# Attention plus feed-forward layer on eight cores: the step between the two halves is split into a statistics pass and a transpose pass

## The reference

```python
x = x + _layernorm(_L0_attn_ref(_layernorm(x), A_l, r_l, B_l, C_l))
x = x + _layernorm(_L0_ffn_ref(_layernorm(x), gate_w, up_w, down_w, ...))

# attention, D = 256 rows of X, the rest Y; N = 2048
U = B_l @ X;  W = C_l @ X
att = relu(U.T @ W);  att[N-1, N-1] = 0
X_out = X + A_l @ (X @ att);  Y_out = Y + r_l * (Y @ att)

# feed-forward, hidden 2048, inner 5632
g = (xf @ gate_w.T) * gate_s;  u = (xf @ up_w.T) * up_s
out = ((silu(g) * u) @ down_w.T) * down_s
```

## Time and profile before

| What | us |
|---|---|
| median of 3 runs | 1420.22 (1420.18 to 1420.74) |
| profiled execution, its own time | 1418.88 |
| its span, slowest core | 1417.3 |
| spans of the eight cores | 1410.9 to 1417.3 |

### The profile page before, as it was taken

The page is one execution under the profiler, slowest core; times in us unless marked ns, Lnnn a source line. Parts: engine busy times, 40 slices in busy tenths (PEclk is TensorE's granted clock), DMA queues, the critical chain, the costliest instruction groups (busy, mean ns, idle before and its releaser), DMA issues. The chain is left out here.

```text
span 1417.3 us, 13080 instructions; the slowest of 8 cores (1410.9 to 1417.3 us)
## 1 busy us (share of the span) xinstructions
PE 1142.3 (81%) x5236; PEld 506.6 (36%) x5236; DVE 372.8 (26%) x487; ACT 239.3 (17%) x316; POOL 46.8 (3%) x68
## 2 busy tenths in 40 slices
PE   2438989931117999999999999999999999999940
PEld 0113333310113444444444444444444444444410
DVE  2066335334330102310123001220113110231285
ACT  2302333355540000000000000000000000000045
POOL 1000000000010000000000000000000000000000
PEclk9769999975558999999999999999999999999975
DMA  6860000002129943085331935137540664303048
GB/s 113 227 129 1 1 1 0 1 30 85 65 78 171 169 87 60 0 139 100 60 60 19 160 61 91 29 59 124 94 80 1 103 124 71 60 0 60 0 141 333
DMA packets 28748, 112.86 MB, mean 80 GB/s; under 512 B 2448, under 2 KB 5008, under 8 KB 24208
## 3 DMA queue, kind: packets, MB, share of 16 engines
q0 software_dynamic: 22784, 75.24, 31.4%
q1 hardware_dynamic: 4752, 33.59, 6.5%
q10 hardware_dynamic: 1152, 3.20, 0.8%
HBM read 170.48 MB, written 16.78 MB: 132 GB/s over the span
## 5 line engine op out<-in xcount | busy, mean ns | idle before, releaser
L752 PE MATMUL ps_f<-att,gw_sb 128*128 128x512 bf16 x1408 | 313.2, 381 | 14.7 <-DMA gw_sb<-gw 14.7
L804 PE MATMUL ps_f<-dwb,hdn 128*128 128x512 bf16 x1408 | 304.9, 379 | 11.7 <-DVE hdn L782 11.7
L768 PE MATMUL ps_f<-att,uw_sb 128*128 128x512 bf16 x1408 | 311.1, 379 | 0.0
L782 DVE SCALAR_TENSOR_TENSOR hdn<-ps_f,us_sb,sg 128x1024 bf16<-128x1024 f32 x44 | 56.5, 1284 | 564.9 <-PE ps_f L768 564.9
L752 PEld LDWEIGHTS ps_f<-att,gw_sb 128*128 128x128 bf16 x1408 | 138.1, 98 | 182.5 <-issue 17.7
L804 PEld LDWEIGHTS ps_f<-dwb,hdn 128*128 128x128 bf16 x1408 | 137.3, 98 | 179.2 <-issue 14.5
L768 PEld LDWEIGHTS ps_f<-att,uw_sb 128*128 128x128 bf16 x1408 | 137.8, 98 | 166.1
L778 ACT ACTIVATE sg<-ps_f,gs_sb 128x1024 bf16<-128x1024 f32 x44 | 49.1, 1115 | 831.6 <-PE ps_f L752 831.6
L425 PE MATMUL ps_t<-att,xTb 128*128 128x512 bf16 x512 | 115.9, 384 | 35.7 <-DMA xTb<-xT 35.7
L817 DVE TENSOR_TENSOR acc<-acc,ps_f 128x2048 f32<-128x2048 f32 x40 | 91.5, 2287 | 172.1 <-PE ps_f L804 172.1
L644 PE MATMUL ps_tr<-ident_sb,xTb 128*128 128x128 bf16 x128 | 16.2, 305 | 108.8 <-ACT xTb L626 105.2
(11 more groups left out here) (104 smaller groups left out, 381.8 us busy)
## 6 DMA issues: line engine op xcount, KB each, us to landing
gw_sb<-gw POOLq DMA_DIRECT2D x22, 1024.0 KB, 8.5
uw_sb<-uw POOLq DMA_DIRECT2D x22, 1024.0 KB, 8.6
dwb<-dw POOLq DMA_DIRECT2D x11, 2048.0 KB, 28.8
xbuf<-x SPq DMA_DIRECT2D x8, 1024.0 KB, 22.4
x1sp<-xbuf SPq DMA_DIRECT2D x8, 1024.0 KB, 3.9
x1rb<-x1sp SPq DMA_DIRECT2D x8, 1024.0 KB, 16.0
y<-acc SPq DMA_DIRECT2D x8, 1024.0 KB, 6.7
xTb<-xT POOLq DMA_DIRECT2D x4, 1024.0 KB, 44.1
```

The lines of the kernel that those rows point to most:

```text
L752: e.matmul(ps_f[:, half, :], gw_sb[:, slot, ht * P:(ht + 1) * P], lnfT_v[:, ht, half * 512:(half + 1) * 512], start=(ht == 0), stop=(ht == ...
L768: e.matmul(ps_f[:, 2 + half, :], uw_sb[:, slot, ht * P:(ht + 1) * P], lnfT_v[:, ht, half * 512:(half + 1) * 512], start=(ht == 0), stop=(h ...
L782: pl.vop(lambda e, gi=gi, li=li: e.scalar_tensor_tensor(hdn[:, li, :], ps_f[:, 2:4, :], us_sb[:, gi:gi + 1], sg[:, gi % 2, :], ALU.mult, A ...
L804: e.matmul(ps_f[:, bs + hc, :], hdn[:, li, tt * P:(tt + 1) * P], dwb[:, li, hc * 512:(hc + 1) * 512], start=(li == 0), stop=(li == blk - 1)),
```

## The change

The step between the halves is taken apart.

- Part of it stays in the second block, without the quarters and without `tmpe`: for each row tile one DVE instruction over 2048 columns computes `xbuf = attn_out * rN8 + xbuf` and its row sum. The constant `ngN8` is left out there (the layernorm that follows doesn't see a constant added to a row) and is added at the end of the kernel, in the bias of the last normalization. The squares are summed as before, the stores too. The statistics `rF` and `ngF8` are made once, for all eight row tiles, after the loop.
- A new block of its own holds the rest. POOL loads the first two chunks of `gw` and `uw` at its start. ACT normalizes a row tile into one of two bf16 tiles `lnfbf`, PE transposes it in the same groups of four, and DVE alone copies all four groups out, into a tile `lnfT` of its own.
- The loads of `dsB` and `dwb` stay in the feed-forward block, which now comes after that block. The condition `blk > 2` ahead of a load holds for all rounds (the rounds have 8 or 4).
- In the fourth block `w1f` is float32 instead of bf16, and one small DVE addition is new. Tiles are placed elsewhere in SBUF and PSUM, with `gw_sb`, `uw_sb` and `lnfT` on its right side.

```diff
-    for dt in range(DT):
-        for c in range(4):
-            pl.aop(... e.activation(tmpe[:, sl, :], attn_out[:, dt, cs_], AF.Identity,
-                scale=rN8[:, dt:dt + 1], bias=ngN8[:, dt:dt + 1]), ...)
-            pl.vop(... e.scalar_tensor_tensor(
-                xbuf[:, dt, cs_], tmpe[:, sl, :], 1.0, xbuf[:, dt, cs_],
-                ALU.mult, ALU.add, accum_out=s1acc[:, dt, c:c + 1]), ...)
+    for dt in range(DT):
+        pl.vop(lambda e, dt=dt: e.scalar_tensor_tensor(
+            xbuf[:, dt, :], attn_out[:, dt, :], rN8[:, dt:dt + 1],
+            xbuf[:, dt, :], ALU.mult, ALU.add,
+            accum_out=s1acc[:, dt:dt + 1]), w=[("sAC", rn_done)])
...
-        pl.vop(lambda e, dt=dt: e.reduce_sum(t1c[:, :], s1acc[:, dt, :], ...))
...
-        pl.aop(lambda e, dt=dt: e.activation(rF[:, dt:dt + 1], lnt[:, dt:dt + 1], AF.Exp, scale=c_nh))
...
+    pl.vop(lambda e: e.tensor_scalar(muF8[:, :], s1acc[:, :], 1.0 / D, None,
+                                     ALU.mult))
+    pl.vop(lambda e: e.tensor_scalar(lnt[:, :], s2acc[:, :], 1.0 / D, None,
+                                     ALU.mult), w=[("sAC", x1sq_ac)])
...
+    pl.aop(lambda e: e.activation(lnt[:, :], lnt[:, :], AF.Ln, bias=c_eps),
+           w=[("sDV", fstat)])
+    pl.aop(lambda e: e.activation(rF[:, :], lnt[:, :], AF.Exp, scale=c_nh))
...
+    pl.new_block()
     load_chunk(0)
     load_chunk(1)
+    for dt in range(DT):
+        pl.aop(lambda e, dt=dt: e.activation(
+            lnfbf[dt % 2][:, :], xbuf[:, dt, :], AF.Identity,
+            scale=rF[:, dt:dt + 1], bias=ngF8[:, dt:dt + 1]), w=wcast)
+        for g4 in range(4):
+            for k in range(4):
+                pl.em("tensor", ... e.transpose(pb[:, k * P:(k + 1) * P],
+                                  lnfbf[dt % 2][:, nt * P:(nt + 1) * P],
+                                  ident_sb[:, :]), ...)
+            pl.vop(lambda e, dt=dt, g4=g4, pb=pb: e.tensor_copy(
+                lnfT[:, g4 * 4:g4 * 4 + 4, dt * P:(dt + 1) * P],
+                pb[:, :].rearrange("p (k c) -> p k c", c=P)), w=[("sPE", tg)])
...
+    pl.emit(nc, sems)
...
+    pl.new_block()
     pl.dma("sDS", "scalar", dsB[:, :], t_ds.ap(), w=[("sSP", SP)])
...
-    w1f = s3.enter_context(nc.sbuf_tensor("w1f", [P, DT, D], BF16))
+    w1f = s3.enter_context(nc.sbuf_tensor("w1f", [P, DT, D], F32))
...
+    pl.vop(lambda e: e.tensor_tensor(ngW8[:, :], ngW8[:, :], ngN8[:, :],
+                                     ALU.add))
```

More of the change, by code:

```diff
@@ L169, in build_nc @@
     nA2 = g_sb("nA2", [P, DT])
+    muW8 = g_sb("muW8", [P, DT])
+    rW8 = g_sb("rW8", [P, DT])
+    ngW8 = g_sb("ngW8", [P, DT])
     cst = g_sb("cst", [P, 2])
@@ L187, in build_nc @@
         nc.sbuf_tensor("amixb", [P, JT, R], BF16, side="right"))
+    sT = ExitStack()
+    attn_out = sT.enter_context(nc.sbuf_tensor("attn_out", [P, DT, D], BF16))
     s0 = ExitStack()
@@ L532, in build_nc @@
         epilogue(1)
[L534 to L540, removed]
     pl.vop(lambda e: e.reduce_sum(muN8[:, :], nacc[:, :, :],
@@ L607, in build_nc @@
[L607 to L663, removed]
@@ L667, in build_nc @@
+    fstat = pl.v("sDV")
+    pl.aop(lambda e: e.activation(lnt[:, :], lnt[:, :], AF.Ln, bias=c_eps),
+           w=[("sDV", fstat)])
+    pl.aop(lambda e: e.activation(rF[:, :], lnt[:, :], AF.Exp, scale=c_nh))
+    rf_done = pl.v("sAC")
+    pl.vop(lambda e: e.tensor_tensor(ngF8[:, :], muF8[:, :], rF[:, :],
+                                     ALU.mult), w=[("sAC", rf_done)])
+    pl.vop(lambda e: e.tensor_scalar_mul(ngF8[:, :], ngF8[:, :], -1.0))
+    ngf_done = pl.v("sDV")
     SP = pl.v("sSP")
@@ L674, in build_nc @@
     sT.close()
[L675 to L687, removed]
+    sTl = ExitStack()
+    lnfT = sTl.enter_context(nc.sbuf_tensor("lnfT", [P, HT, R], BF16,
+                                            side="right"))
+    sW2 = ExitStack()
+    gw_sb = sW2.enter_context(nc.sbuf_tensor("gw_sb", [P, 4, D], BF16,
+                                             side="right"))
+    uw_sb = sW2.enter_context(nc.sbuf_tensor("uw_sb", [P, 4, D], BF16,
+                                             side="right"))
     g_mm_done = {}
@@ L707, in load_chunk @@
         uw_ld[ci] = (usem, pl.v(usem))
+    sTx = ExitStack()
+    lnfbf = [sTx.enter_context(nc.sbuf_tensor(f"lnfbf{i}", [P, D], BF16))
+             for i in range(2)]
+    psT = ExitStack()
+    ps_tr = [psT.enter_context(nc.psum_tensor(f"ps_tr{i}", [P, 4 * P], BF16))
+             for i in range(2)]
     pl.new_block()
@@ L711, in build_nc @@
     load_chunk(1)
+    tr_done = {}
+    ev_done = {}
+    for dt in range(DT):
+        wcast = []
+        if dt >= 2:
+            wcast.append(("sPE", tr_done[dt - 2]))
+        pl.aop(lambda e, dt=dt: e.activation(
+            lnfbf[dt % 2][:, :], xbuf[:, dt, :], AF.Identity,
+            scale=rF[:, dt:dt + 1], bias=ngF8[:, dt:dt + 1]), w=wcast)
+        cast_done = pl.v("sAC")
+        for g4 in range(4):
+            pb = ps_tr[g4 % 2]
+            wt = [("sAC", cast_done), ("sXI", XI)]
+            prev = (dt, g4 - 2) if g4 >= 2 else ((dt - 1, g4 + 2)
+                                                 if dt > 0 else None)
+            if prev in ev_done:
+                wt.append(("sDV", ev_done[prev]))
+            for k in range(4):
+                nt = g4 * 4 + k
+                pl.em("tensor",
+                      lambda e, dt=dt, nt=nt, k=k, pb=pb:
+                      e.transpose(pb[:, k * P:(k + 1) * P],
+                                  lnfbf[dt % 2][:, nt * P:(nt + 1) * P],
+                                  ident_sb[:, :]),
+                      w=(wt if k == 0 else ()),
+                      inc=("sPE" if k == 3 else None))
+            tg = pl.v("sPE")
+            pl.vop(lambda e, dt=dt, g4=g4, pb=pb: e.tensor_copy(
+                lnfT[:, g4 * 4:g4 * 4 + 4, dt * P:(dt + 1) * P],
+                pb[:, :].rearrange("p (k c) -> p k c", c=P)),
+                w=[("sPE", tg)])
+            ev_done[(dt, g4)] = pl.v("sDV")
+        tr_done[dt] = pl.v("sPE")
+    pl.emit(nc, sems)
+    sTx.close()
+    sx.close()
+    psT.close()
+    s2 = ExitStack()
+    acc = s2.enter_context(nc.sbuf_tensor("acc", [P, DT, D], F32))
+    dsB = s2.enter_context(nc.sbuf_tensor("dsB", [P, D], F32))
+    s2w = ExitStack()
+    dwb = s2w.enter_context(nc.sbuf_tensor("dwb", [P, 8, D], BF16))
+    hdn = s2w.enter_context(nc.sbuf_tensor("hdn", [P, 8, R], BF16))
+    sg = s2w.enter_context(nc.sbuf_tensor("sg", [P, 2, R], BF16))
+    ps2 = ExitStack()
+    ps_f = ps2.enter_context(nc.psum_tensor("ps_f", [P, 8, MQ], F32))
+    pl.new_block()
     pl.dma("sDS", "scalar", dsB[:, :], t_ds.ap(), w=[("sSP", SP)])
@@ L727, in build_nc @@
             load_chunk(ci0)
-            load_chunk(ci0 + 1)
+            if blk > 2:
+                load_chunk(ci0 + 1)
         wdw = ([("sPE", down_mm[(bi - 1, 6)])] if bi > 0
@@ L753, in build_nc @@
                                    gw_sb[:, slot, ht * P:(ht + 1) * P],
-                                   lnfT_v[:, ht, half * 512:(half + 1) * 512],
+                                   lnfT[:, ht, half * 512:(half + 1) * 512],
                                    start=(ht == 0), stop=(ht == HT - 1)),
@@ L825, in build_nc @@
     s2w.close()
+    sW2.close()
+    sTl.close()
     s3 = ExitStack()
     x1rb = s3.enter_context(nc.sbuf_tensor("x1rb", [P, DT, D], F32))
-    w1f = s3.enter_context(nc.sbuf_tensor("w1f", [P, DT, D], BF16))
+    w1f = s3.enter_context(nc.sbuf_tensor("w1f", [P, DT, D], F32))
     pl.new_block()
```

53 lines of the change are left out of this document (14 added, 39 removed).

## The result

The changed kernel takes 1350.2 us (median of 8 runs, 1349.1 to 1351.5), against 1420.2 for the kernel before, measured beside it. Some executions show a lower granted clock on the cores of one die and take longer; the times and ratios here are of the others. The ratio is 0.9509, with an interval from 0.9498 to 0.9520: faster by 4.9%. I had forecast 1344.5 and a range from 1339 to 1349, so the direction is right, the gain is smaller than forecast (70 us in place of 76), and the time lies 1.2 us above the range. The profiled execution took 1351.0 us with a span of 1349.4; its slowest core is core 2.

The account below looks back on a forecast made before the run. The step from 303 us was taken as a chain between engines, ahead of a matmul-bound feed-forward; starting that 76.0 us earlier, with 0.3 us added at the end, gave 1420.2 - 75.7 = 1344.5 us, range 1339 to 1349.

Parts of the forecast that it names:

- What bounds the kernel now: Feed-forward bound by matmuls; 303 to 421 us a chain passing between engines, then only DMAs work until 434.6.
- The statistics pass: DVE's eight merged instructions of 2.35 us and four of line 592: 29.4 us in all, to 332.7.
- the statistics at once: Statistics for all row tiles after the loop, a chain on 8 columns: 2.45 us, to 335.2.
- A new block end: After the statistics: 0.34 us from DVE's last instruction to ACT's first, 0.71 to POOL's; ACT starts at 335.5.
- The weights: First `gw` chunk, asked for at 335.9, lands at 349.3, 9 us ahead of need; the 14.72 us wait vanishes.
- The transpose pass: PE starts at 337.8; 16 pairs of groups at 1.25 us each; last copy ends at 358.2.
- The end: Fourth block: one small DVE instruction and its gap, +0.27 us; float32 `w1f` costed at nothing.
- the length of the feed-forward: Feed-forward instructions left alone; growth beyond PE's 927 us, by clock or a chunk wait, would make the prediction wrong.
- Warm transposes: Rival, chance 0.22: PE's clock rises within the transpose pass, saving 1.8 us there and 2.1 at feed-forward start: 1340.6.
- Late weights: Rival, chance 0.07: weight loads and DVE's copies exclude each other; loads land at 362.9, 4.3 us late: 1348.8.
- Slower than before: Rival, chance 0.02: lower granted clock in the feed-forward; gain eaten at mean clock 0.925, at 0.90 it gives 1447.

Follow-up runs that it names:

- four buffers: Four PSUM buffers for the transposes instead of two, against the changed kernel: ratio 0.9512, 1351.0 us; the same edit was also made on the one-block version.
- one-block version with four buffers: Attention, statistics, transposes and feed-forward in one block, `w1f` bf16, and four PSUM transpose buffers instead of two, against the changed kernel: ratio 0.9437, 1340.3 us.
- one-block version: Attention, statistics, transposes and feed-forward in one block joined by semaphores, `w1f` bf16 again, against the changed kernel: ratio 0.9467, two executions, 1344.1 and 1345.4 us.

## Why the prediction was wrong

The stretch on the profiled core was to be 358.6 - 303.07 = 55.5 us and was 63.8. Step by step:

- *What bounds the kernel now*, the chain through the engines: right. Each row tile's chain is gone and so is the wait for `gw_sb`.
- *The statistics pass* and *the statistics at once*: right to a tenth. The merged instruction took 2.35 us, and from the start of `ngN8` to the end of both steps it was 32.1 us as forecast. A bf16 operand beside a float32 one didn't double the rate.
- *A new block end*: this is the step that failed, with 6.6 of the 8.3 us. I took its price of 0.4 us from block ends at which POOL's loads had long landed, and put it at both ends of the new block. The second waits for POOL's loads to land and cost 5.67 us from the last copy to PE. The experiments show this from four sides: less to land, no gap; more to land for nobody, a longer gap; no block end, no gap; an earlier last copy, a gap longer by as much. The trace of the kernel before held it, in no row of mine: in its second block POOL's `DRAIN` lasted until the loads of `xTb` had landed (40.6 + 52.9 = 93.5 us, and 41.6 + 51.8 = 93.4), and it cost nothing only because the block went on to 420 us. The head of the block brought ACT's table load, 1.28 us. The trace before has four blocks and four such loads, one at the head of ACT's work in each, and I didn't count them. The rows of POOL's `DRAIN` and loads before:

```profile
L74 POOLq DRAIN  x1: 52887/52887/52887, 40.6 to 40.6; - x1
...
L66 POOL DMA_DIRECT2D xTb<-xT x4: 757/765/780, 39.4 to 41.6; - x4
...
DMA to landing us min/median/max: 26.2/44.1/51.8
```

- *The weights*: the sum that they are in time for PE was right, and it was the wrong question. I asked when the first chunk is needed and not who else waits for the last of them. The loads' bandwidth was in my rows (166 GB/s in the earlier trace rows); at that rate four transfers of 1 MB take 25.3 us by my estimate, so from POOL's start at 335.9 to 361.2, behind the last copy that I forecast for 358.2.
- *The transpose pass*: the mechanism was right, the size off. A pair took 1.33 us and not 1.25 (the first 1.68), and the whole pass 22.1 instead of 20.4. The term was the signal from PE to DVE: I took 0.17 us from a second group, and the first group's, which is in the loop, takes 0.26 (340.80 + 0.50 to 341.56), near the 0.23 that I had read for ACT.
- *The end* and the length of the feed-forward: right within a microsecond. First gate matmul to line 829 took 930.1 us, against 929.5 before; the fourth block 0.6 us more where I had 0.3.
- 6.6 and 1.7 make the 8.3 us. The attention part of the profiled core ended 1.35 us earlier than before, which is luck and hides part of the miss; the feed-forward added 0.7 and the end 0.3. That makes 7.9, and the profiled execution is off by 1351.0 - 1343.2 = 7.8. The median is off by less, 5.7, since the profiled execution was 1.3 under the median before and is 0.8 above it now.

The rivals. *Warm transposes* didn't happen: the granted clock is 0.50 (1.2 GHz) throughout the pass, on all eight cores. It does happen with four buffers. *Late weights* gave about the right time (1348.8) for another reason: beside DVE's copies the loads moved 165 GB/s, as before with DVE idle (166), and no product of PE waited for them. The Trainium skill's rule that POOL can't write its descriptors while DVE runs in a two-port mode ("SBUF — State Buffer", "SBUF: two separate sides") had no case here, since the copies read PSUM. The four requests, of 0.70 to 0.74 us each, came before the first copy and test nothing. In the one-block version with four buffers two requests for `dwb` fall within the copies; they took 1.51 us together, as in the changed kernel with DVE idle. *Slower than before*: the clock in the feed-forward stayed at 1.00. The Trainium skill's limiter of 1.95 GHz, which stands in the section "Seeing it yourself" of "TensorE: Matmul & The Clock Gate" and not in the one that I named, doesn't show in it.

Open: the traces name the instruction that waits, POOL's `DRAIN`, but not why it waits for landings where SP's doesn't. Whether ACT's queue would be waited for was not tried, nor whether the table load comes with the block's head alone or with whatever ACT runs first in it.

## What to carry to other kernels

A barrier has as its price not the 0.4 us that a quiet one shows, but the latest of everything it waits for: here all DMAs asked for by POOL since the block began. The duration of POOL's `DRAIN` in the trace shows it ahead of any change, also where it costs nothing yet. Loads moved ahead to hide them must either land before the barrier or be asked for behind it, and the second chunk, which isn't needed at once, belongs behind it. Before a stage is made faster, look which wait ends last at its end: four buffers gave nothing in one version and 4 us in the next.

## What the runs showed that I had not expected

- The end of a block waited for POOL's DMAs to land, to within 0.4 to 0.5 us in four traces (364.9 and 365.38; 365.9 and 366.37; 379.5 and 380.01; 369.4 and 369.81), and did not wait for SP's. What waits is the `DRAIN` in POOL's queue.
- ACT loads a table of 1.28 us at the head of each block that uses it: four before, five in the changed kernel, four again without the second block end. There the table load in front of `Silu` is gone, and one at line 651 serves both. The one-block version has four in three blocks, one of them in front of `Silu`.
- With four buffers the granted clock rises within the transposes, on all eight cores, in the changed kernel as in the one-block version. On core 1 of the one-block version with four buffers the windows read as follows, and its first 32 gate matmuls took 7.07 us instead of 8.41 in the changed kernel:

```profile
340.00:345.00 5.00, 3.67 (x37) 3.14 (x36) 4.07 (x10) 4.72 (x4) 0.00 (x0) 0.64 1.00 413
345.00:350.00 5.00, 3.69 (x40) 3.17 (x39) 3.84 (x10) 4.81 (x3) 1.51 (x2) 0.71 0.38 83
350.00:356.00 6.00, 3.03 (x43) 2.52 (x40) 4.86 (x12) 3.28 (x2) 0.00 (x0) 0.96 0.96 177
```

In the changed kernel with its two buffers PE is busy for a larger part of the time, 8.49 of 10 us, and the clock stays at 0.50. What decides between the two stays open.
